# Local attention: the order of the stacking transfers, and what the first scores wait for

## The reference, cut to what matters

```
DIM, DEPTH, HEADS, DIM_HEAD, WINDOW = 128, 2, 8, 64, 64
def _layer(x, wqkv, qs, ksc, wo, ...):
    h = shift_token(x)                       # half of the features come from the token before
    q, k, v = split(h @ wqkv, 3)             # 8 heads of 64
    q = l2norm(q) * qs
    k = l2norm(k) * ksc
    q, k = rotary_xpos(q, k)                 # rotates each head's two halves of 32
    o = local_attention(q, k, v)             # windows of 64 queries see their own and the previous 64 keys
    x = x + o @ wo
    ...                                      # then a gated feed-forward
```

## Time and profile before

| | |
|---|---|
| three timed runs | 8472.45, 8457.02, 8474.06 us, median 8472.45 |
| profiled execution | span 8469.3 us, first to last instruction; no other time is listed for it |
| TensorE clock, mean of the span | 0.808 of 2.4 GHz |
| busy share of the span | PE 72%, PEld 36%, DVE 50%, ACT 36%, POOL 23% |
| the four attention calls (first stacking DMA to last scores of its last batch's first unit, roughly) | 5233 to 5656, 5816 to 6236, 7304 to 7725 and 7885 to 8308 us |

### The profile page before, as it was taken

One profiled execution on the slowest core, in us unless ns is written; L12 is line 12 of the kernel. 1 busy time (PEld: TensorE's weight loads), 2 busy tenths in 40 slices (PEclk: granted clock), 3 DMA queues, 4 the chain that ended last, 5 costly groups with the idle time before them and its releaser, 6 DMA issues. The chain is left out here.

```text
span 8469.3 us, 123982 instructions
## 1 busy us (share of the span) xinstructions
PE 6094.0 (72%) x46161; PEld 3016.1 (36%) x46352; DVE 4274.2 (50%) x6846; ACT 3054.3 (36%) x6729; POOL 1907.5 (23%) x1689
## 2 busy tenths in 40 slices
PE   5557567876678876665789997777776666677677
PEld 3445251115432222222345443443443333344343
DVE  4324436653357647888544444444445555444444
ACT  1002323553335614433112223553543333354453
POOL 0112042113232104444110001432420000242341
PEclk6558677887778987877868878998997777899898
DMA  1001013211111000000032221111100000110110
GB/s 42 4 32 46 22 55 77 66 53 52 57 54 39 26 14 0 0 0 0 7 60 51 51 50 29 37 30 41 37 23 7 0 0 0 36 38 24 45 39 23
DMA packets 261149, 269.25 MB, mean 32 GB/s; under 512 B 113472, under 2 KB 190657, under 8 KB 258689
## 3 DMA queue, kind: packets, MB, share of 16 engines
q1 hardware_dynamic: 250368, 240.70, 11.0%
q0 software_dynamic: 10240, 21.25, 0.8%
HBM read 123.03 MB, written 71.66 MB: 23 GB/s over the span
## 5 line engine op out<-in xcount | busy, mean ns | idle before, releaser
L2170 PE MATMUL ps<-s_l2b_hc,ident 128*128 128x512 f32 x512 | 362.2, 847 | 331.9 <-DVE s_l2b_hc L2333 331.9
L1942 DVE TENSOR_REDUCE s_l3l_negmax<-ps 128x4 f32<-128x512 f32 x256 | 175.0, 684 | 743.3 <-PE ps L1783 743.3
L2118 POOL TENSOR_TENSOR s_l2b_Bx<-s_l2b_du,s_l2b_B 128x512 f32<-128x512 f32 x256 | 406.6, 1610 | 473.9 <-ACT s_l2b_B L2240 411.0
L1783 PE MATMUL ps<-s_l3l_qk 64*64 64x64 f32 (+1 forms) x5632 | 298.0, 256 | 287.1 <-DMA s_l3l_qk<-s_l3l_rope 267.9
L1873 ACT ACTIVATE s_l3l_probs<-ps,s_l3l_biases,s_l3l_q_inverse 128x128 f32<-128x128 f32 x1024 | 455.6, 462 | 53.0 <-DVE s_l3l_biases L1944 52.6
L2325 DVE TENSOR_TENSOR_SCAN s_l2b_state<-s_l2b_decay,s_l2b_Bx 128x512 f32<-128x512 f32 x256 | 390.0, 1563 | 155.2 <-ACT s_l2b_decay L2246 113.3
L1721 POOL TENSOR_TENSOR s_l3l_probs<-s_l3l_probs,s_l3l_inverse 128x512 f32<-128x512 f32 x256 | 267.1, 1043 | 828.6 <-DVE s_l3l_inverse L1923 828.4
L1745 PE MATMUL ps<-s_l3l_hs,s_l3l_wqk 128*128 128x512 f32 x512 | 304.3, 702 | 177.8 <-DVE s_l3l_prod L1897 95.4
L1057 DVE TENSOR_REDUCE s_L3a_negmax<-ps 128x1 f32<-128x128 f32 (+3 forms) x512 | 236.2, 488 | 345.6 <-PE ps L893 343.1
L638 DVE TENSOR_REDUCE s_L1a_negmax<-ps 128x1 f32<-128x512 f32 x512 | 316.6, 682 | 149.0 <-PE ps L501 148.2
L1035 ACT ACTIVATE s_L3a_pt<-ps 128x256 f32<-128x256 f32 (+3 forms) x512 | 195.3, 434 | 513.3 <-PE ps L893 511.5
(11 more groups left out here) (654 smaller groups left out, 14161.8 us busy)
## 6 DMA issues: line engine op xcount, KB each, us to landing
s_l3l_qk<-s_l3l_rope SPq DMA_DIRECT2D x1024, 64.0 KB
scratch_rope<-s_L3a_rope SPq DMA_DIRECT2D x32, 512.0 KB, 2.8
ks<-scratch_parts SPq DMA_DIRECT2D x384, 32.0 KB
s_L3a_qs<-scratch_rope SPq DMA_DIRECT2D x64, 128.0 KB
ks<-scratch_rope SPq DMA_DIRECT2D x64, 128.0 KB
s_L0e_slots<-scratch_sent SPq DMA_DIRECT2D x16, 396.0 KB, 5.6
s_L1e_slots<-scratch_sent SPq DMA_DIRECT2D x16, 396.0 KB, 5.7
scratch_square<-s_L1a_rows SPq DMA_DIRECT2D x24, 256.0 KB, 3.0
```

The lines of the kernel that those rows point to most:

```text
L1783: mm = pe.matmul(out[rows, P * k + at:P * k + at + size], t["qk"][rows, b % 2, c, 64 * m:64 * m + 64], t["qk"][rows, b % 2, 4 + c, key:key ...
L2118: pool.tensor_tensor(t["Bx"][:, n % 2, k, :], t["du"][:, b % 2, k, :], t["B"][:, n % 2, :], ALU.mult).then_inc(s["bx_ready"], 1)
L2170: pe.matmul(ps[:, 4 + k, :], g["ident"][:, :], t["hc"][:, n % 2, k, :], start=(n == 0), stop=(n == STATES - 1)).then_inc(s["summed"], 1)
```

## The change

It has two parts. SP issues the stacking DMAs in the order tile 0, 2, 1, 3 (query, key, query, key) in place of 0, 1, 2, 3. And `stacked` becomes two semaphores, one for the even tiles (head pairs 0, 1) and one for the odd ones (head pairs 2, 3): PE waits for the even one before unit 0 and for the odd one before unit 4; POOL's rotation waits for that of its tile; SP waits for both.

```diff
-    names = ("... rows_floored rows_ready stacked v_shifted "
+    names = ("... rows_floored rows_ready stacked_even stacked_odd v_shifted "
...
-        STACKED = 16 * 32
+        STACKED = 16 * 16
...
             for b in range(BATCH):
-                sp.wait_ge(s["stacked"], START + b * STACKED)
+                sp.wait_ge(s["stacked_even"], START + b * STACKED)
+                sp.wait_ge(s["stacked_odd"], START + b * STACKED)
                 if b > 1:
                     sp.wait_ge(s["scores_ready"], START + (b - 1) * UNITS)
-                for e in range(4):
+                for e in (0, 2, 1, 3):
                     if e < 2:
                         sp.wait_ge(s["rope_made"], START + 8 * b + 2 * e + 2)
                     else:
                         taken(sp, ("pick", b, e - 2))
...
-                            sp.dma_start(t["qk"][...], t["rope"][...]).then_inc(s["stacked"], 16)
+                            sp.dma_start(t["qk"][...], t["rope"][...]).then_inc(s["stacked_odd" if e % 2 else "stacked_even"], 16)
...
-                pool.wait_ge(s["stacked"], START + b * STACKED)
+                pool.wait_ge(s["stacked_odd" if e % 2 else "stacked_even"], START + b * STACKED)
...
                 if u == 0:
-                    pe.wait_ge(s["stacked"], START + (b + 1) * STACKED)
+                    pe.wait_ge(s["stacked_even"], START + (b + 1) * STACKED)
+                if u == 4:
+                    pe.wait_ge(s["stacked_odd"], START + (b + 1) * STACKED)
```

More of the change, by code:

```diff
@@ L1596, in local_attention @@
                "probs": ([P, LAG + 1, 4, P], F32), "turned": ([P, 2, T], F32), "o": ([P, PAIRS, T], F32)}
-    names = ("loaded pool pool_ready tables_ready shifted ready6 ready7 taken6 taken7 squared rope_made rows_floored rows_ready stacked v_shifted "
+    names = ("loaded pool pool_ready tables_ready shifted ready6 ready7 taken6 taken7 squared rope_made rows_floored rows_ready stacked_even stacked_odd v_shifted "
              "scores_ready found max_ready exp_ready inverse_ready probs_ready turned_ready turned_taken pv_done o_taken")
@@ L1673, in _ @@
                             at = 64 * r + 32 * ab
-                            sp.dma_start(t["qk"][at:at + 32, b % 2, 4 * (e // 2) + c, :], t["rope"][32 * k:32 * k + 32, e, ab, :]).then_inc(s["stacked"], 16)
+                            sp.dma_start(t["qk"][at:at + 32, b % 2, 4 * (e // 2) + c, :], t["rope"][32 * k:32 * k + 32, e, ab, :]).then_inc(s["stacked_odd" if e % 2 else "stacked_even"], 16)
         @block.gpsimd
```

## The result

The changed kernel takes 8324.31 us (median of 4 runs, 8302.09 to 8330.69) against 8472.85 us (4 runs): 148.5 us less, ratio 0.9823 with a 95% interval of 0.9807 to 0.9839. Run once more on another occasion it gave 0.9815 (0.9788 to 0.9841). The forecast was 8310 with a range of 8276 to 8336.

The account below looks back on a forecast made before the run. The prediction took unit 0's scores to be held up by SP's one-by-one stacking DMA issues. From 8469.3 it took 162 us (32 x 5.07), all else nothing, giving 8307, or 8310 for the median; range 8276 to 8336.

Parts of the forecast that it names:

- What bounds unit 0: Unit 0's scores wait on SP's issue of 16 DMAs; waiting for eight fewer saves 5.07 us per batch, 162 us.
- The 0.36: Share of the stacking burst in which DMA engines were read as busy, so SP's issue was the limit.
- Nothing else is late: After the shorter wait, even tiles still come last at unit 0, with 3.3 us of stall left per batch.
- Unit 4: Its scores wait for the odd tiles, now last in the burst: 18.0 us to spare, costed at nothing.
- The rotation of tile 1: POOL's work for the next batch, behind the later tile 1 stacking: 6.8 us to spare, costed at nothing.
- the DMA named as releaser there before: Trace's releaser of POOL's rotation, 48 times, 78.2 us; claimed that DVE's product was the real wait.
- The added semaphore waits: Two more per batch on PE, SP and POOL: costed at nothing, at most 0.65 us per batch (21 us).
- The order: Tile 1's eight issues move behind tile 2 into a burst of 24; costed at nothing.
- The clock: TensorE's clock falls in the stall before unit 0; expected to remain so, zero taken, from 54 us gained to 104 lost.
- a distance that shrinks by less than the wait: Sign of a wrong forecast: batch distance falling less than PE's wait, pointing to the clock or the chain of units.
- the clock stays up: Rival: TensorE's clock holds in the shortened stall before unit 0, gain 162 + 54, 8256 us; chance 0.06.
- reaches over unit 1 as well: Rival: 24 DMAs in flight or low clock over unit 1 give back up to 104 us, middle 8360; chance 0.05.

Follow-up runs that it names:

- e1: Kernel before the change, with only the new tile order 0, 2, 1, 3 and its one semaphore kept: 8661.99 us, one run, against 8485.2 us.
- e2: Changed kernel with its two semaphores but the old tile order 0, 1, 2, 3: 8328.45 us, ratio to before 0.9813.
- e4: Changed kernel with PE's mask matmul of unit 0 ahead of the wait and nine more, overwritten masks before it: 8265.52 us, ratio 0.9734.
- e6: Kernel before the change, with PE's mask of unit 0 ahead of the wait and thirty more, overwritten masks: 8417.97 us, ratio 0.9945.
- e7: Changed kernel with one semaphore per head pair, old tile order, first pair's four transfers first in tile 2: 8177.56 us, ratio 0.9649.

## Why the prediction was right

*What bounds unit 0.* Right. From the first issue of the key tile's burst to the first score's weight load it was 12.44 us before and 7.38 after (means of 32): 5.06 us where 5.07 was forecast. e1 shows the same price with the other sign. The 0.36 that the prediction read as the DMA engines' share during the burst is that of its end alone, from 5316.30 on; from the first issue to the end of the last, 5309.01 to 5319.38, it is 0.37, so nothing changes by it. The Trainium skill, page DMA: Bandwidth & Descriptors, section "Issuing engines are not separate DMA queues", holds that starting a DMA is usually small beside the DMA itself. For these transfers the trace disagrees: eight issues less were worth 5.06 us, while the DMA engines were busy 0.38 of the new burst (5317.86 to 5333.46).

*Nothing else is late.* Right. The wait behind the stall is still that for the transfers. Unit 4 had 18.4 us to spare (last issue ended at 5333.46, with the 1.97 us of landing 5335.4, against 5353.82). The POOL timeline answers to the earlier trace rows:

```profile
5342.67 1.27 POOL L1699 TENSOR_TENSOR s_l3l_rope<-s_l3l_prod 128x512 f32<-128x512 f32 x1 [1.48 <-DVE s_l3l_prod L1900]
```

The rotation of tile 1 follows DVE's product, 7.2 us after its own stacking landed. That the DMA named as releaser there before was not the cause was right too: its idle time is the same 1.48 us with another name beside it. Over the span the view of the tile `rope` has all of the rotations' idle time behind DVE now,

```profile
  DVE s_l3l_prod L1900: 224.3, 128
```

where before it was 146.0 us (80 times) behind DVE and 78.2 (48 times) behind the DMA, 224.2 together. The added semaphore waits cost nothing that shows: units 3 to 7 take the same time as before to 0.02 us.

*The order.* I costed it at nothing and e2 shows nothing. The prediction could have gone further: it did not say that the order is not needed for the gain, although the rows showed it, since tile 2 was already first in the burst.

*The clock.* This is the term that was mis-sized, within its bounds. I took zero, expecting the fall to remain, and gave the range more room below because a shorter stall would rather help the clock. The fall remained, but the low stretch moved, and the shorter stall did not help. In the 28 batches that follow another, the granted clock fell 5.87 us ahead of the products' first weight load before and rose 3.76 us after it; with the change it falls 1.33 us ahead (in three of them only after) and rises 4.76 us after. So less of the low stretch lies in the stall and more on the work. What makes it rise later is not shown. Unit 0 takes 5.91 us (6.02 in the second trace) in place of 5.55: 11.5 us over 32 batches. With it the sum is 162 - 11.5 = 150.5, and the calls gave 152.0. The distance, 4.84 us shorter where the path of the transfers is 5.06 shorter, shows the same: a distance that shrinks by less than the wait was named as a sign that points at the clock. The rivals in which the clock stays up, or reaches over unit 1 as well, did not come true: unit 1 to unit 2 is 5.59 us after and 5.53 before.

*The distance between 8310 and 8324.* Of these 14 us the calls have 10 (162 forecast, 152.0 measured), about what the clock took. The other 4 lie outside the calls, in stages that the change does not touch, where the traces of one kernel and another differ by up to 35 us.

## What to carry to other kernels

Count the issues between the event that allows a transfer and the work that needs it: where one queue starts many small transfers, a finer semaphore is worth the issues that it takes out, and the consumer should wait for exactly what its first piece reads (here four transfers of 32). Before reordering, look which of them are already first in the burst. When a stall of TensorE is shortened and not removed, price the clock behind it from rows on both sides: the low stretch can move onto the work.

## What the runs showed of the hardware that was not expected

A stall of 2.9 us left the granted clock low for longer in the work behind it (4.52 us of unit 0) than one of 8.4 us (3.71 us): it had fallen 1.33 us before the work in the one case and 5.87 us before it in the other. The length of the stall does not order this by itself, since one of 13.6 us (e1) left 4.22 us. With idle stretches of 1.4 us between matmuls (e4, e6), and with what is left of the stall in e7, the clock stayed at 2.4 GHz in nearly all batches (0.00, 0.21 and 0.47 us of low clock in unit 0). A DMA of 64 KB between two places of the on-chip memory cost SP 0.63 us from one issue to the next (median), with the DMA engines busy 0.3 to 0.5 of the time; 24 in a row took 15.60 us, 0.65 each.
